# Packing the probability-times-V matmuls as three whole tiles instead of four half tiles

## The reference

```python
h = (x - mu) * lax.rsqrt(var + 1e-05) * ln_gamma + ln_beta
qkv = (h @ w_qkv + b_qkv).reshape(B, T, 3, NUM_HEADS, HEAD_DIM)
...
scores = jnp.einsum('bhqd,bhkd->bhqk', q, k) / np.sqrt(HEAD_DIM)
attn = jax.nn.softmax(scores, axis=-1)
out = jnp.einsum('bhqk,bhkd->bhqd', attn, v)
```

## Time and profile before

| what | value |
|---|---|
| three timed runs | 2784.02, 2787.62, 2787.01 us; median 2787.01 us |
| profiled execution | 2784.02 us, of it 2782.2 us span |
| attention 0 | from the start to about 737 us of the span |
| TensorE matmul busy, whole span | 2669.8 us (96%) |
| VectorE busy, whole span | 2395.7 us (86%) |
| ScalarE busy, whole span | 2030.0 us (73%) |
| mean granted TensorE clock | 0.985 |

### The profile page before, as it was taken

How to read it: one execution, slowest core, us unless ns; L and a number is a source line. 1 busy time by engine, 2 the same in 40 slices (tenths; PEclk the granted TensorE clock), 3 DMA queues, 4 the chain that set the end, 5 groups by cost and what they waited for, 6 DMA issues and landing times.

```text
span 2782.2 us, 49559 instructions
## 1 busy us (share of the span) xinstructions
PE 2669.8 (96%) x18215; PEld 2018.5 (73%) x18215; DVE 2395.7 (86%) x4300; ACT 2030.0 (73%) x4473; POOL 1489.3 (54%) x1083
## 2 busy tenths in 40 slices
PE   7999999999999999999999999999999999999996
PEld 3444444444577777888888898888898888888895
DVE  7999999999588877787888888888888988888987
ACT  2888888888665556777777777777777777777773
POOL 3303113000255555676776766776766786766763
PEclk7999999999999999999999999999999999999998
DMA  4120111200221210000000000000000000000000
GB/s 134 38 82 31 60 46 44 83 17 18 81 81 34 66 62 8 1 1 1 1 1 3 3 1 3 3 1 3 3 3 1 3 3 1 3 3 1 3 3 6
DMA packets 41330, 65.42 MB, mean 24 GB/s; under 512 B 5176, under 2 KB 15992, under 8 KB 41088
## 3 DMA queue, kind: packets, MB, share of 16 engines
q1 hardware_dynamic: 41088, 62.26, 6.9%
HBM read 45.86 MB, written 15.86 MB: 22 GB/s over the span
## 4 chain that ended last, share of the span: by engine, by line
PE 60%; DVE 28%; issue 6%; ACT 4%; POOL 2%; SPq 0%; DMA 0%; DVEq 0%; ACTq 0%; POOLq 0%
PE P L1872 16%; PE P L1897 9%; PE P L1734 7%; PE P L1695 7%; DVE a_mx L1264 6%; DVE c_nm L1430 6%; PE P L1883 5%; PE P L1801 4%; DVE c_DT L1455 4%; PE P L1906 3%; PE P L1812 2%; PE P L1855 2%; DVE c_Tl L1463 1%; DVE d_tc L1538 1%; DVE b_hf L1356 1%
## 5 line engine op out<-in xcount | busy, mean ns | idle before, releaser
L1430 DVE TENSOR_REDUCE c_nm<-P 128x1 f32<-128x1024 f32 x512 | 622.1, 1215 | 108.0 <-PE P L1872 106.8
L962 ACT ACTIVATE c_P<-P,c_nm 128x1024 f32<-128x1024 f32 x512 | 571.9, 1117 | 182.1 <-DVE c_nm L1430 181.4
L1264 DVE TENSOR_REDUCE a_mx<-P 128x1 f32<-128x512 f32 x1024 | 622.7, 685 | 11.2 <-PE P L1695 10.6
L2098 POOL TENSOR_TENSOR c_P<-c_P,c_P 128x1024 f32<-128x1024 f32 (+1 forms) x256 | 617.4, 2412 | 21.3
L832 ACT ACTIVATE a_PT<-P 128x512 f32<-128x512 f32 x976 | 523.0, 596 | 85.5 <-PE P L1707 69.7
L2096 POOL TENSOR_SCALAR c_P<-c_P,c_rr 128x1024 f32<-128x1024 f32 (+1 forms) x256 | 297.0, 1160 | 444.3 <-DVE c_rr L1442 444.2
L1897 PE MATMUL P<-c_DT,c_xkh 128*128 128x256 f32 x2048 | 390.4, 284 | 2.7 <-DVE c_DT L1455 2.7
L1872 PE MATMUL P<-c_xth,c_Th 128*128 128x512 f32 x1024 | 365.9, 438 | 18.0 <-ACT c_P L962 18.0
L1455 DVE TENSOR_TENSOR c_DT<-P,c_DT 128x512 fp32r<-128x512 f32 x512 | 348.5, 681 | 9.2 <-ACT c_DT L973 8.8
L1695 PE MATMUL P<-a_Ks,a_Qs 32*128 32x512 f32 x1024 | 327.0, 515 | 9.4 <-DMA a_Qs<-qk_scratch 6.6
L1734 PE MATMUL P<-a_PT,a_Vp 128*32 128x256 f32 (+1 forms) x4000 | 327.4, 399 | 8.5 <-ACT a_OT L847 8.2
(11 more groups left out here) (245 smaller groups left out, 5187.8 us busy)
## 6 DMA issues: line engine op xcount, KB each, us to landing
b_cwB<-cw_scratch SPq DMA_DIRECT2D x64, 256.0 KB, 4.9
qk_scratch<-a_nh SPq DMA_DIRECT2D x32, 256.0 KB, 3.1
a_Ks<-qk_scratch SPq DMA_DIRECT2D x32, 256.0 KB, 3.1
a_Qs<-qk_scratch SPq DMA_DIRECT2D x32, 256.0 KB, 3.9
c_stg<-in_cw SPq DMA_DIRECT2D x8, 640.0 KB, 3.8
qk_scratch<-a_nl SPq DMA_DIRECT2D x16, 256.0 KB, 3.6
b_stg<-in_moe SPq DMA_DIRECT2D x9, 384.0 KB, 3.2
out<-xres SPq DMA_DIRECT2D x15, 128.0 KB, 1.8
```

What stands on the lines that cost most here:

```text
L962: e.activation(m.P1[s][n % 4][:, :], P[:, k:k + 2, :].rearrange("p c k -> p (c k)"), ACT.Exp, bias=m.nm[:, n % 4, s:s + 1], accum_out=m.sm ...
L1264: e.tensor_reduce(m.mx2[u % 2][:, t // 4, j, t % 4, half:half + 1], bank("maxima", u, t, j, half), AX, ALU.max).then_inc(m.S["a_max_dve"])
L1430: e.tensor_reduce(m.nm[:, n % 4, s:s + 1], P[:, k:k + 2, :].rearrange("p c k -> p (c k)"), AX, ALU.max, negate=True).then_inc(m.S["c_nm"])
L2098: e.tensor_tensor(p0, p0, p1, ALU.add).then_inc(m.S["c_D"])
```

## The change

`bursts` now takes the unpaired tiles of a half in the order in which their scores are made, and cuts them into groups of three, each tile with all 512 queries. A full half of 32 tiles gives ten bursts of three tiles and one of two, 11 in place of 16. (The first half of the last unit, 16 unpaired tiles, gives four of three and one of four.) Each tile is one matmul instead of two. A burst is due 6 slots behind its last tile, so that there is one every three slots. Behind a burst up to two steps of `behind` are put, not one.

```diff
 def bursts(u, c):
-    cuts = []
-    for hs in range(8 * c, 8 * c + 8):
-        tiles = [(hs, (i + 2) % 4) for i in range(4)]
-        cuts += [(tiles, 0, 512)] if paired(u, hs) else [(tiles, 0, 256), (tiles, 256, 512)]
-    return cuts
+    waves = [[(hs, (i + 2) % 4) for i in range(4)] for hs in range(8 * c, 8 * c + 8)]
+    tiles = [t for w in waves for t in w if not paired(u, t[0])]
+    whole = [w for w in waves if paired(u, w[0][0])]
+    rest = len(tiles) % 3
+    last = 4 if rest == 1 else rest
+    cuts = [tiles[k:k + 3] for k in range(0, len(tiles) - last, 3)] + [tiles[len(tiles) - last:]] * bool(last)
+    return cuts + whole
...
-        for k, (tiles, first, _) in enumerate(cuts):
+        for k, tiles in enumerate(cuts):
             hs, j = tiles[-1]
-            due.setdefault(4 * (16 * u + hs) + (j + 2) % 4 + SUM_LAG + 2 * bool(first), []).append(("burst", u, c, k))
+            due.setdefault(4 * (16 * u + hs) + (j + 2) % 4 + SUM_LAG, []).append(("burst", u, c, k))
...
-                for step in behind[:1]:
+                for step in behind[:2]:
                     put(step)
-                behind = behind[1:]
+                behind = behind[2:]
...
-        tiles, first, end = BURSTS[u, c][k]
-        for hs, j in tiles:
+        for hs, j in BURSTS[u, c][k]:
...
-            tt = e.matmul(O[32 * j:32 * j + 32, first:end], m.Vp[b % 2][:, at_v:at_v + 32], m.PT[:, j, hs % 4, first:end],
-                          start=(kt == 0 and first == 0), stop=(kt == 7 and end == 512))
+            tt = e.matmul(O[32 * j:32 * j + 32, :], m.Vp[b % 2][:, at_v:at_v + 32], m.PT[:, j, hs % 4, :],
+                          start=(kt == 0), stop=(kt == 7))
```

More of the change, by code:

```diff
@@ L50, in bursts @@
 def bursts(u, c):
-    cuts = []
-    for hs in range(8 * c, 8 * c + 8):
-        tiles = [(hs, (i + 2) % 4) for i in range(4)]
-        cuts += [(tiles, 0, 512)] if paired(u, hs) else [(tiles, 0, 256), (tiles, 256, 512)]
-    return cuts
+    waves = [[(hs, (i + 2) % 4) for i in range(4)] for hs in range(8 * c, 8 * c + 8)]
[5 more added lines that the diff above has]
+    return cuts + whole
 BURSTS = {(u, c): bursts(u, c) for u in range(NU) for c in range(2)}
-BURST_OF = {(u, *t): (u, c, k) for (u, c), cuts in BURSTS.items() for k, (tiles, _, _) in enumerate(cuts) for t in tiles}
+BURST_OF = {(u, *t): (u, c, k) for (u, c), cuts in BURSTS.items() for k, tiles in enumerate(cuts) for t in tiles}
 def half_sums(u, c):
```

## The result

The changed kernel takes 2803.27 us (median of 4 runs, 2800.89 to 2803.63) against 2785.52 us for the kernel before on the same chip: ratio 1.0063, 95% interval 1.0048 to 1.0079. That is 17.8 us more; the forecast was 17. The page of the changed kernel, the rows that answer to the earlier trace rows and the row of the bursts. (PE is TensorE's matmuls, PEld its weight loads, DVE VectorE, ACT ScalarE, POOL GpSimd; in brackets stand the idle time before a row and what ended it.)

The account below looks back on a forecast made before the run. VectorE was taken to bound the clean stretches, mostly TensorE the projection stretches; 8 us plus 8.4 us, some 17 us, on the 2787 us median gave 2804 us (own range 2793 to 2814; full range 2790 to 2834).

Parts of the forecast that it names:

- The pace before: Stretches without projections, kernel before: VectorE sets the pace, 19.85 us for a half of 32 slots.
- the waits of line 1695 for VectorE should shrink: Sign expected in the changed kernel's profile: line 1695 waits less for VectorE; no size given.
- Burst 1.00 us, third slot 0.23 us: TensorE in attention 0: a burst of three whole tiles takes 1.00 us, a group's third slot adds 0.23 us.
- the first rival: Third slot served after the first in full, 0.43 us: TensorE's half 20.8 us, 43 us slower, 2830 us; chance 0.27.
- TensorE's half, 18.8 us: TensorE's own work in a half after the change: 18.8 us, 1.0 under VectorE's 19.85.
- The loop through three banks, 1.81 us a group: Scores waiting for ScalarE's three banks: 3.62 us for two groups, 1.81 for one, against VectorE's 1.80.
- Clean stretches, 8 us: Stretches without projections: 25.5 halves lose 0.3 us each, 8 us (0 to 18).
- Projection stretches, 8.4 us: Three stretches with the next batch's projections: TensorE's 53 slots take 2.8 us more in each, 8.4 us in all.
- cover: none: Projection stretches: VectorE is idle 10% there, so none of TensorE's added time is hidden.
- The waits for the copy to `OT`: Line 1734's 17.8 us of waits over 30 halves would end, giving nothing back in the clean stretches.
- VectorE hides it all: Rival: banks take up every disturbance, and ScalarE and VectorE set the projections' pace; 0 to 5 us more, 2789 us; chance 0.16.
- faster: Rival: a three-tile burst costs less than one of four, 0.79 us, gaining in projection stretches; 2781 us; chance 0.06.

Follow-up runs that it names:

- the two other engines light: Changed kernel with the exponential of only 256 of 512 queries and the maxima of only 256 of 512 keys; 2759.26 us (one run), clean half 19.18 us.
- VectorE light: Changed kernel with VectorE reducing only the first 256 of the 512 keys of a tile; 2786.04 us, clean half 20.17 us.
- ScalarE light: Changed kernel with the exponential of only 256 of the 512 queries, which the burst multiplies twice; 2794.74 us, clean half 19.96 us.

## Why the prediction was right

- **The pace before** (VectorE in the clean halves, 19.85 us): right by its chain and its share of busy time. The third ground, TensorE's 56 waits for VectorE, says little, as shown above; and the sign "the waits of line 1695 for VectorE should shrink" did not come either (21.4 us before, 27.1 after, in the same stretch).
- **Burst 1.00 us, third slot 0.23 us**: measured 0.99 and 0.23. These two decided between the forecast and the rivals. The rule of the Trainium skill that was weighed here (TensorE: Matmul & The Clock Gate, Part 3, The mechanism: a load overlaps only if its row group differs) does not agree with the load at 608.89 above, which lies under a matmul of its own row group. The measurement decides, and it decides against the first rival. (That rival's excess is 20.82 - 19.85 = 0.97 us a half, not 0.93, so 25 us and not 24; nothing hangs on it.)
- **TensorE's half, 18.8 us**: 19.18 with the two other engines light; `row2`'s group takes 0.55 us extra and not 0.20. It fits under 19.85 as said.
- **The loop through three banks, 1.81 us a group**: the step on which the forecast turned, and the one that the runs support best. 3.62 us for two groups in the changed kernel, 20.17 us a half with VectorE light, 2.64 us a group in the variant with four tiles, worse with less work for TensorE. The loop through VectorE's four banks seems nearly as tight: with ScalarE light 0.11 of the 0.40 us stays.
- **Clean stretches, 8 us**: mis-sized low. 0.3 us a half were taken, midway between two bounds and not worked out; the plain ones lost 0.40, and four with `out_project` 1.2 each, a step that the sum had left out (610.43 to the next slot at 611.52 is 1.09 us of TensorE). Over all intervals but those of the projections (nine of them) it is 19.1 - 8.3 = 10.9 us. VectorE's idle time in the clean stretch came as TensorE's doing but at 0.6 us a half (5.0 us in 164), not 0.3.
- **Projection stretches, 8.4 us**: 8.3 us over the nine intervals (9.5 at an equal clock), but this is a right total by luck. The step "cover: none" failed: with bursts of two tiles the interval with the projections grew by 3.9, not 6.9, and with four whole tiles, which need less of TensorE, it got longer. And the two held steps save 7.3 us there (6 on the kernel's time), which the prediction had at nothing, since there would seldom be two at once; at 166.33 and 167.15 there are. So two errors cancel: with one held step the loss would have been 15.6 us, and the second step gives 7.3 back. Half of what was forecast rests on this.
- **The waits for the copy to `OT`** were to end. They went from 17.8 us to 10.6 and are still there in all 30 halves; no gain from it shows.
- **The clock** was put at full in all these stretches. The earlier trace rows has 0.96 from 490 to 530 us, which is worth the 1.2 us above.
- **From 737 us on** nothing was to change: from the last copy of bank 4 to the end it is 2044 us before and 2045 after.
- The rival "VectorE hides it all" fell by the 20.25 us; "faster" fell by the 0.99 us of a burst, whether of three tiles or of two.

The mechanism of the clean stretches is therefore right, and its size low; around the projections only the size is right.

## What to carry to other kernels

When three engines are all nearly full, add up not only each one's work but each loop through a ring of buffers: consumer latency, consumer time, producer time, divided by what the ring holds. A long step on the producer that comes more rarely can lose although its total is smaller: what counts is how many buffers are used between two such steps, and whether the last of them is the first one again. Here, with three banks, three slots to a burst cost 0.4 us a half and four 2.1. And when the points in a schedule at which held steps are put get rarer, look at the steps that wait for them.

## What was not expected of the hardware

- A float32 burst on column tiles took the time of its columns and not of its tiles: 0.98 to 1.00 us for two, three or four tiles of 512 columns, 0.57 for four of 256.
- Matmuls for row groups that were still streaming had their loads hidden (608.89 above) and put the burst off by only 0.23 us, the spacing of matmuls on all rows.
- The idle time of TensorE's loads behind a burst (0.41 us before, 0.84 after) was put down to VectorE even in the run in which VectorE waited for TensorE.
